# Cross-attention output projection in 28 tiles of 128 tokens instead of 32 tiles of 112, with the loop over batches written out

## What is computed

```python
q = proj(hs, Wq, bq, S); k = proj(at, Wk, bk, T); v = proj(at, Wv, bv, T)
scores = jnp.einsum('bhsd,bhtd->bhst', q, k) / scale
probs = jax.nn.softmax(where(attend, clip(scores), -50), axis=-1)
ctx = jnp.einsum('bhst,bhtd->bhsd', probs, v).transpose(0, 2, 1, 3).reshape(B, S, H)
delta = rs * (ctx @ Wo.T + bo)
delta = layernorm(delta) * ln_gamma + ln_beta
x = layernorm(x + delta)
# the feed-forward part then needs max|x| over the whole tensor, for its scale
```

## Time and profile before

| what | value |
|---|---|
| median of 3 runs | 1490.15 us (1488.83 to 1490.62) |
| the profiled execution | 1488.81 us, span 1487.0 us |
| PE busy | 1440.3 us, 97% of the span |
| DVE busy | 1055.3 us, 71% |
| ACT busy | 656.9 us, 44% |
| POOL busy | 579.2 us, 39% |
| cross-attention | from about 390 to 1262 us of the span |
| granted PE clock, mean | 0.991 of full speed |

### The profile page before, as it was taken

How to read it: one execution, slowest core, us unless ns; L and a number is a source line. 1 busy time by engine, 2 the same in 40 slices (tenths; PEclk the granted TensorE clock), 3 DMA queues, 4 the chain that set the end, 5 groups by cost and what they waited for, 6 DMA issues and landing times. The chain is left out here.

```text
span 1487.0 us, 33650 instructions
## 1 busy us (share of the span) xinstructions
PE 1440.3 (97%) x13322; PEld 1123.5 (76%) x13322; DVE 1055.3 (71%) x2021; ACT 656.9 (44%) x865; POOL 579.2 (39%) x510
## 2 busy tenths in 40 slices
PE   7899999999899999999999999999999996899898
PEld 3688888887788888888888888888888885455343
DVE  2866565564477777877777778777787777677898
ACT  1333333333343343433433433334333332789996
POOL 0000000000144544555445545454545453753576
PEclk9999999999999999999999999999999998899999
DMA  6023333321511212112111121121111210439895
GB/s 219 29 79 103 103 103 102 102 76 52 184 41 42 73 45 72 39 45 72 45 47 64 45 72 39 45 72 45 56 55 45 72 46 24 107 113 327 274 348 200
DMA packets 80743, 138.59 MB, mean 93 GB/s; under 512 B 5218, under 2 KB 52834, under 8 KB 78898
## 3 DMA queue, kind: packets, MB, share of 16 engines
q1 hardware_dynamic: 80690, 137.87, 28.4%
HBM read 93.82 MB, written 44.04 MB: 93 GB/s over the span
## 5 line engine op out<-in xcount | busy, mean ns | idle before, releaser
L737 POOL TENSOR_TENSOR xa_psum<-xa_pr 125x448 f32<-125x448 f32 x126 | 153.9, 1221 | 236.3 <-DVE xa_pr L883 236.3
L883 DVE TENSOR_SCALAR xa_pr<-xa_pr,xa_keep 125x448 f32<-125x448 f32 x384 | 151.0, 450 | 108.3 <-ACT xa_pr L783 107.0
L783 ACT ACTIVATE xa_pr<-xa_bSC 125x1344 f32<-125x1344 f32 x128 | 165.6, 1293 | 138.3 <-PE xa_bSC L989 132.3
L764 ACT ACTIVATE xa_kf<-xa_bKV,xa_bk 128x376 f32<-128x376 f32 x128 | 73.6, 575 | 184.9 <-PE xa_bKV L913 184.9
L740 POOL TENSOR_TENSOR xa_psum<-xa_psum,xa_pr 125x448 f32<-125x448 f32 x126 | 147.0, 1167 | 12.1 <-POOL xa_psum L737 4.4
L913 PE MATMUL xa_bKV<-left_xn,wA 128*128 128x376 f32 x768 | 149.9, 344 | 0.0
L913 PE MATMUL xa_bKV<-xa_cx,wA 128*128 128x376 f32 x768 | 149.3, 343 | 0.0
L770 ACT COPY xa_v<-xa_bKV 125x512 f32<-125x512 f32 x96 | 56.2, 585 | 206.2 <-PE xa_bKV L924 201.1
L924 PE MATMUL xa_bKV<-wZ,left_xn 128*125 128x512 f32 x576 | 141.9, 394 | 1.7 <-POOL xa_ones L713 1.7
L924 PE MATMUL xa_bKV<-wZ,xa_cx 128*125 128x512 f32 x576 | 141.1, 393 | 0.0
L913 PEld LDWEIGHTS xa_bKV<-left_xn,wA 128*128 128x128 f32 x768 | 130.0, 188 | 8.9 <-issue 5.3
(11 more groups left out here) (193 smaller groups left out, 2508.8 us busy)
## 6 DMA issues: line engine op xcount, KB each, us to landing
wraw<-in_ctxT SPq DMA_DIRECT2D x32, 752.0 KB, 4.8
ff_hr<-h_scratch SPq DMA_DIRECT2D x28, 512.0 KB, 6.5
wraw<-in_w SPq DMA_DIRECT2D x8, 1024.0 KB, 7.7
sa_raw<-in_x SPq DMA_DIRECT2D x8, 896.0 KB, 5.9
x_scratch<-left_qraw SPq DMA_DIRECT2D x8, 896.0 KB, 5.1
xa_qf<-q_scratch SPq DMA_DIRECT2D x32, 224.0 KB, 4.9
xa_x<-x_scratch SPq DMA_DIRECT2D x32, 224.0 KB, 4.7
x_scratch<-xa_x SPq DMA_DIRECT2D x32, 224.0 KB, 2.3
```

Source lines behind the costliest of these rows:

```text
L737: nc.gpsimd.tensor_tensor(psum01[:], third(h, 0), third(h, 1), ALU.add).then_inc(p01_ok, 1)
L783: nc.scalar.activation(pr[h][:], bSC[0:TW, :, 0:TC * S], ACT.Exp, scale=XSCALE).then_inc(exp_ok, 1)
L883: nc.vector.tensor_scalar(third(h, t), third(h, t), EM50, bound, ALU.max, ALU.min).then_inc(pr_ok, 1)
```

## The change

The tokens of all batches are now treated as one row of 32 x 112 = 3584, cut into 28 tiles of 128. `cT` becomes a ring of two tiles (256 columns). `attended` writes its 112 columns where they belong in the ring; where they run over the end of it they are written in two pieces, which is so in 12 of the 32 batches (2, 4, 6, 9, 11, 13 and the same plus 16). Tile t is projected after the batch that completes it. No tile is completed by the batches 0, 8, 16 and 24, so no output and no tail stands in the batches 1, 9, 17 and 25. In these four, the third part of the values moves from h = 0 to h = 1. The tail works on 128 rows. The row maxima go to a tile `rows`, and at the end they are gathered into four columns of `amax`. All 32 batches are written out on every engine.

```diff
+        def tile_of(b):
+            return b - 1 - b // 8 if b >= 0 and b % 8 else None
+        def pieces(b):
+            lo = b * S % (CR * P)
+            n0 = min(S, CR * P - lo)
+            return [(0, n0, lo)] + ([(n0, S - n0, 0)] if n0 < S else [])
+        def third_value(b):
+            return 1 if b % 8 == 1 else 0
+        def every(body):
+            for b in range(B):
+                body(b, b % 2, b // 2)
...
-        cT = [n.sb(f"cT{i}", [P, C, S], F32R) for i in range(2)]
+        CR = 2
+        cT = [n.sb(f"cT{i}", [P, C, CR * P], F32R) for i in range(2)]
...
-                wait(sp, x2_out[par], 8 * (b - par))
-                sp.dma_start(x1[par][:], x1_d[b]).then_inc(x1_in[par], 16)
+                t = tile_of(b)
+                if t is not None:
+                    wait(sp, x2_out[t % 2], 16 * (t // 2))
+                    sp.dma_start(x1[t % 2][:], x1_v[t]).then_inc(x1_in[t % 2], 16)
...
-                    wait(dve, o_done, b)
-                nc.vector.tensor_scalar(cT[0][:, h, :], at[:], bvt[:, h:h + 1], None, ALU.add).then_inc(cthi_ok, 1)
+                    wait(dve, o_done, ((b + 1) * S - 1) // P - CR + 1)
+                for lo, size, to in pieces(b):
+                    hi = nc.vector.tensor_scalar(cT[0][:, h, to:to + size], at[:, lo:lo + size], bvt[:, h:h + 1], None, ALU.add)
+                hi.then_inc(cthi_ok, 1)
                 dve.wait_ge(cthi_ok, s + 1)
-                nc.vector.scalar_tensor_tensor(out=cT[1][:, h, :], in0=at[:], scalar=bvt[:, h:h + 1],
-                                               in1=cT[0][:, h, :].bitcast(F32), op0=ALU.add, op1=ALU.subtract).then_inc(ctlo_ok, 1)
+                for lo, size, to in pieces(b):
+                    low = nc.vector.scalar_tensor_tensor(out=cT[1][:, h, to:to + size], in0=at[:, lo:lo + size], scalar=bvt[:, h:h + 1],
+                                                         in1=cT[0][:, h, to:to + size].bitcast(F32), op0=ALU.add, op1=ALU.subtract)
+                low.then_inc(ctlo_ok, 1)
...
-                nc.vector.tensor_reduce(amax[:, bass.ds(b, 1)] if not isinstance(b, int) else amax[:, b:b + 1], x1[par][:], AX_X, ALU.max,
+                nc.vector.tensor_reduce(rows[:, t:t + 1], x1[t % 2][:], AX_X, ALU.max,
...
-            tail2(B - 1, 1)
-            tail3(B - 1, 1)
+            dve.wait_ge(amax_ok, NT - 1)
+            nc.vector.tensor_reduce(top[:], rows[:, 0:NT - 1], AX_X, ALU.max).then_inc(top_ok, 1)
+            tail2(NT - 1)
+            dve.wait_ge(top_ok, 6)
+            row_maxima(0, top)
+            tail3(NT - 1)
+            dve.wait_ge(amax_ok, NT)
+            row_maxima(2, rows[:, NT - 1:NT])
...
-                        mm = nc.tensor.matmul(bKV[1][0:S, 0:D], cT[l][:, c, :], w["o"][r][:, c, :],
+                        mm = nc.tensor.matmul(bKV[1][:, 0:D], cT[l][:, c, own], w["o"][r][:, c, :],
...
-                    if h == 0:
+                    if h == third_value(b):
                         values(b, par, 2)
-                    elif h == 1:
-                        if not first(b):
-                            output(b - 1)
-                    elif not last(b):
+                    if h == 1 and tile_of(b - 1) is not None:
+                        output(b - 1)
+                    if h >= 2 and not last(b):
                         values(b + 1, 1 - par, h - 2)
...
-            steps(pe, body, B, 2)
+            every(body)
```

More of the change, by code:

```diff
@@ L663, in cross_attention @@
         NFIRST, NSMALL = 4, 3
+        Q3 = 3 * HD
         def last(b):
@@ L740, in body @@
                         nc.gpsimd.tensor_tensor(psum[h % 2][:], psum01[:], third(h, 2), ALU.add).then_inc(ps_ok, 1)
[L741 to L750 removed]
+                    if h == 0 and tail is not None:
+                        x1_beta(tail)
+                    if h == 1 and tail is not None:
+                        norm(tail)
+            every(body)
+            x1_beta(NT - 1)
+            norm2(NT - 2)
+            norm(NT - 1)
+            norm2(NT - 1)
         @block.scalar
@@ L872, in tail3, with row_maxima @@
                                         apply_absolute_value=True).then_inc(amax_ok, 1)
+            def row_maxima(column, of):
+                nc.vector.tensor_copy(amax[0:Q3, column:column + 1], of[0:Q3])
+                nc.vector.tensor_copy(amax[0:P - Q3, column + 1:column + 2], of[Q3:P])
             def body(b, par, pair):
+                tail = tile_of(b - 1)
                 for h in range(C):
@@ L877, in body @@
                         split_low(b + 1, 1 - par)
-                    if h == 3 and not first(b) and not last(b):
-                        tail2(b - 1, 1 - par)
+                    if h == 3 and tail is not None and not last(b):
+                        tail2(tail)
                     dve.wait_ge(exp_ok, 4 * b + h + 1)
@@ L886, in body @@
                         attended(b - 1, C - 1)
-                    if h == 1 and not first(b):
-                        tail1(b - 1)
+                    if h == 1 and tail is not None:
+                        tail1(tail)
                     if h == 2:
@@ L894, in body @@
                         output_weights(h)
-                    if h == 3 and not first(b) and not last(b):
-                        tail3(b - 1, 1 - par)
-            steps(dve, body, B, 2)
+                    if h == 3 and tail is not None and not last(b):
+                        tail3(tail)
+            nc.vector.memset(amax[:], 0.0)
+            every(body)
             attended(B - 1, C - 2)
             attended(B - 1, C - 1)
-            tail2(B - 2, 0)
-            tail1(B - 1, mv1, st1)
-            tail3(B - 2, 0)
-            tail2(B - 1, 1)
-            tail3(B - 1, 1)
+            tail2(NT - 2)
+            tail1(NT - 1, mv1, st1)
+            tail3(NT - 2)
+            dve.wait_ge(amax_ok, NT - 1)
[6 more added lines that the diff above has]
+            row_maxima(2, rows[:, NT - 1:NT])
         @block.tensor
```

132 lines of the change are left out of this document (66 added, 66 removed).

## The result

| what | before | after |
|---|---|---|
| median | 1490.38 us (4 runs, 1488.83 to 1491.41) | 1481.22 us (4 runs, 1481.08 to 1484.86) |
| ratio of the times | | 0.9948 (95%: 0.9931 to 0.9965) |
| profiled execution | 1488.81 us, span 1487.0 | 1484.86 us, span 1483.1 |
| first scores of batch 0 | 393.53 us | 396.69 us |
| first to last scores of the stage | 851.71 us | 843.51 us |

What follows compares the result with a forecast made beforehand. The prediction took PE to set the time of the cross-attention stage. Open slots -8.2, wait for `psum` +0.8 and end +0.6 summed to -6.8 us, from 1490.15 to a median of 1483.4 us, range 1480.6 to 1488.0 us.

Steps and rivals of the forecast that it cites:

- The open slots: Batches 1, 9, 17 and 25, h = 0, without output projection: 2.06 us saved each, 8.2 us less in all.
- The wait for `psum`: At h = 2 of those four batches PE waits 0.2 us for POOL's `psum`, 0.8 us back in all.
- the clamps of h = 1 won't come earlier with the scores: DVE's clamps stand behind two `attended` and `split_low`, so won't come 2 us earlier; PE is then 0.12 us early.
- The end: End of the cross-attention stage, DVE on the path to `amax`: 0.6 us more, between 0.3 and 0.9 us.
- The top reduction: DVE's added reduction of 27 columns ahead of the last `tail2`, at the stage's end: 0.2 us more.
- The last copies: Two one-column DVE copies behind the last reduction: 0.15 us each, with a wait of about 0.1 us before them.
- The split pieces: `cT` written in two pieces in 12 batches: 0.6 us per `attended` pair (0.4 to 1.0), nothing in time.
- Rival (1): Added pieces wait for POOL; PE stands 1.7 us in each of 10 split batches, time 1500 us; chance 0.06.
- Rival (2): Same meeting of pieces with POOL, weaker: stalls of 0.1 to 0.45 us in 10 batches, 1484.5 to 1488 us; chance 0.13.
- The loop written out: Batches 2 to 29 run without a branch but instructions must be fetched; nothing taken for both.
- rival (3): Loop's branch stalls, 1.2 us each, saved 14 times: 17 us less, time 1466 us; chance 0.04.
- Rival (4): PE stands as long in the open slots as the filler took: no gain, about 1490 us; chance 0.06.

## Why the prediction was right

**The open slots** were right in kind and size: 4 x 2.06 us. What made the size right was to read the slot from batch 0, where the filler was already missing, and not from the 2.95 us of the matmuls. With the latter the term would have been 11.8 us. The filler put back returned all of it.

**The wait for `psum`** was mis-sized: 0.8 us in the sum, none in the rows. The step that failed is the sentence that the clamps of h = 1 won't come earlier with the scores, since DVE had been idle for only 0.17 us before them. They came 0.67 us earlier in the batch (9.37 us after its first scores, against 10.04 in the ordinary batch 12). The 0.17 us is one part. The other is that DVE's chain ahead of them ends 0.42 us earlier once the batches are written out, which I had priced at nothing because I looked only at PE's pace. Even without the move of the values there is no wait: written out, the room is 2.17 us instead of 2.03, the slot takes 2.06 of them, and 0.12 us were measured. The mechanism itself is real: with the keys first, where PE comes earlier and the clamps later, the wait appears with 0.3 us.

**The end** is 0.74 us in the rows where 0.6 was forecast, but for reasons that are mostly others. The top reduction cost its 0.2 us. The last copies, 0.4 us of the term with their wait, cost nothing, since all engines wait there until SP, with its last store, is done; the term took DVE for the last one, which it isn't. Instead the clamps of the last batch met POOL's addition of beta and took 1.04 us more, of which 0.52 us reached the last output. This cause is read from two neighbouring rows and was not tried by itself.

**The split pieces** cost PE nothing, as forecast, though they took more than I had given: a pair loses up to 0.7 us of room at h = 3 and up to 1.2 us at h = 1, where the prediction took 0.6, with bounds of 0.4 to 1.0. The room, which at h = 3 is also 0.3 us larger than in the kernel before, held them. Rival (1) described meetings that do occur; what failed is their number at the one place where they would count. Rival (2) had the same form and didn't come either.

**The loop written out** cost and brought PE nothing, which rules out rival (3): 851.70 against 851.71 us for the stage. By the Trainium skill (Runtime: NRT & Kernel Launch, Instruction fetch mechanics) a taken branch out of the fetched window stalls. This trace shows no such stall: from 500 to 1200 us the loop had no instruction fetched at all, so the rule's case did not arise, and PE lost no time. Rival (4), no gain at all, fell with the first row of the slots.

The sum in the rows is -7.46 us against -6.8. The medians differ by 9.2 us, and the repeat with five runs by 8.5, at intervals of 2 to 3 us either way; what is beyond the rows can't be told from the spread.

## What to carry to other kernels

Read what a removed piece is worth from a place in the same trace where it is already missing. It also shows which wait ends the slot when the piece is gone, here 0.66 us for the keys, and 2.06 instead of 2.95 us saved. A margin that was measured in a loop holds for the loop: written out, the engines that are not the bound can run ahead by some tenths of a microsecond at unchanged pace, and small waits worth a fraction of a microsecond can appear or vanish by that alone.

## What was unexpected of the hardware

- POOL's power on one column took 2.08 us in the kernel before and 0.99 us in the changed one, at the same place in the tail. The row count and the loop were ruled out. One of the kernel before took 1.03 us, where DVE's clamps began 0.05 us later beside it.
- An added small DVE instruction right behind one of the same kind costs 0.13 us, and not the 0.15 us that a lone one shows. Beside POOL the same pair of instructions took 1.23 to 2.34 us.
- From DVE's last reduction to its first instruction in the next program block it is 0.85 us in three kernels, and two small copies fit into it unseen. SP, with its store behind the same reduction, is the last engine to end the block.
- 66 blocks of instructions were fetched during the stage with no effect on PE's pace.
